# Second routing of a two-layer mixture-of-experts kernel: the four experts of a token from sorted maxima, experts innermost

## The reference, cut to what matters

```python
# _L1_ffn_ref, E = 16, K = 4
logits = hidden_states @ router_w + router_b
probs = jax.nn.softmax(logits, axis=-1)
topw, topi = jax.lax.top_k(probs, K)
topw = topw / jnp.sum(topw, axis=-1, keepdims=True)
combine = jnp.sum(jax.nn.one_hot(topi, E, dtype=hidden_states.dtype) * topw[..., None], axis=2)
...
def body(acc, expert):
    w1e, b1e, w2e, b2e, ce = expert
    hmid = jax.nn.gelu(x @ w1e + b1e, approximate=False)
    return (acc + (hmid @ w2e + b2e) * ce[:, None], None)
```

## Time and profile before

| what | value |
|---|---|
| median of 3 runs | 1959.16 us (1958.06 to 1961.44) |
| the profiled execution | 1959.49 us, its span 1957.8 us |
| PE busy | 1644.8 us, 84% of the span |
| DVE busy | 1159.4 us, 59% |
| ACT busy | 1079.9 us, 55% |
| POOL busy | 659.6 us, 34% |
| second routing, first to last DVE instruction | 1285.03 to 1359.78 us |
| the experts after it, last `join` | to some 1915 us, to 1957.8 us |

### The profile page before, as it was taken

One profiled execution on the slowest core, in us unless ns is written; L12 is line 12 of the kernel. 1 busy time (PEld: TensorE's weight loads), 2 busy tenths in 40 slices (PEclk: granted clock), 3 DMA queues, 4 the chain that ended last, 5 costly groups with the idle time before them and its releaser, 6 DMA issues. The chain is left out here.

```text
span 1957.8 us, 33224 instructions
## 1 busy us (share of the span) xinstructions
PE 1644.8 (84%) x9891; PEld 1111.1 (57%) x9892; DVE 1159.4 (59%) x1934; ACT 1079.9 (55%) x2236; POOL 659.6 (34%) x622
## 2 busy tenths in 40 slices
PE   4989999561699599999999999824999999999990
PEld 2333343250599455444444444512999999999990
DVE  6999998488411264458999999367233333333325
ACT  5888987540133243138887788614455555555554
POOL 0000000130366231211333333211577777777750
PEclk9999999785699799989999999965999999999995
DMA  5000000134121296503333433186344444444427
GB/s 177 1 0 1 0 1 0 47 120 139 41 66 58 85 317 247 71 18 78 78 99 99 100 99 105 33 280 234 53 70 73 68 71 70 65 67 69 69 23 257
DMA packets 145735, 173.67 MB, mean 89 GB/s; under 512 B 29139, under 2 KB 110430, under 8 KB 145504
## 3 DMA queue, kind: packets, MB, share of 16 engines
q1 hardware_dynamic: 104160, 128.29, 21.7%
q0 software_dynamic: 33248, 43.71, 12.8%
q10 hardware_dynamic: 8224, 0.39, 0.2%
HBM read 111.50 MB, written 66.19 MB: 91 GB/s over the span
## 5 line engine op out<-in xcount | busy, mean ns | idle before, releaser
L1323 PEld LDWEIGHTS f_ht_ps<-f_XT,f_WS 128*128 128x128 f32 x2912 | 357.0, 194 | 15.0 <-DVE f_WS L1416 2.6
L1323 PE MATMUL f_ht_ps<-f_XT,f_WS 128*128 128x128 f32 x2912 | 359.9, 277 | 3.0 <-ACT f_XT L1364 3.0
L1331 PE MATMUL f_y_ps<-W,f_HT 128*128 x1456 | 344.1, 379 | 0.0
L1289 POOL DMA_INDIRECT moe<-f_Y,TOK x182 | 276.8, 1521 | 182.6 <-ACT f_Y L1389 146.5
L2151 DVE TENSOR_REDUCE att_MX<-att_s_ps 128x2 f32<-128x1024 f32 x256 | 304.5, 1216 | 53.2 <-PE att_s_ps L1915 53.0
L2116 ACT ACTIVATE att_PT<-att_st_ps 128x512 f32<-128x512 f32 x512 | 278.7, 594 | 69.7 <-PE att_st_ps L1940 59.5
L1331 PEld LDWEIGHTS f_y_ps<-W,f_HT 128*128 128x128 f32 x1456 | 262.6, 190 | 28.3
L1280 POOL DMA_INDIRECT XG<-x,TOK x182 | 191.9, 1054 | 196.2 <-issue 126.0
L1416 DVE COPY f_WS<-W 128x1024 f32 x182 | 133.4, 733 | 203.3 <-PE f_ht_ps L1323 126.3
L1424 DVE TENSOR_TENSOR f_Y<-f_y_ps,f_B 128x256 f32<-128x256 f32 x143 | 60.7, 425 | 296.4 <-PE f_y_ps L1331 296.4
L303 PE MATMUL rec_ring<-rec_XC,rec_W 128*128 128x512 f32 x384 | 183.6, 632 | 50.8 <-DVE rec_XC L353 21.5
(11 more groups left out here) (276 smaller groups left out, 2198.9 us busy)
## 6 DMA issues: line engine op xcount, KB each, us to landing
W<-in_w SPq DMA_DIRECT2D x48, 512.0 KB, 10.0
att_Q<-qk_pairs SPq DMA_DIRECT2D x192, 64.0 KB, 2.9
att_K<-qk_pairs SPq DMA_DIRECT2D x192, 64.0 KB, 2.9
qk_pairs<-prj_HI SPq DMA_DIRECT2D x16, 512.0 KB, 3.8
qk_pairs<-prj_LO SPq DMA_DIRECT2D x16, 512.0 KB, 5.1
hidden<-in_xT SPq DMA_DIRECT2D x8, 512.0 KB, 7.8
x<-n_Y SPq DMA_DIRECT2D x8, 512.0 KB, 3.0
prj_X<-x SPq DMA_DIRECT2D x8, 512.0 KB, 9.1
```

Of the source, the lines that this page charges most:

```text
L1289: nc.gpsimd.indirect_dma_start(out=outs[n % len(outs)], out_offset=bass.IndirectOffsetOnAxis(ap=TOK[:, n:n + 1], axis=0), in_=Y[n % R][:], ...
L1323: mm = nc.tensor.matmul(ht_ps[r % 2][:, f * P:(f + 1) * P], WS[r % 2][:, at:at + P], XT[r % 2][:, c], start=(c == 0), stop=(c == DC - 1))
L1331: mm = nc.tensor.matmul(y_ps[r % 2][:], HT[r % 2][:, f], W2[:, bass.ds(e * W_EXPERT + f * D, D)], start=(f == 0), stop=(f == FC - 1))
```

## The change

Only the K = 4 path of `route` is rewritten; K = 1 keeps its instructions. The probabilities, the masks and the counts are now stored with the token tile outside and the expert inside (`PJ`, `GJ`, `TJ`, `NJ`, `SJ`, `KEEPJ`, shape `[P, TILES, E]`).

- In place of the four rounds, 32 `max` instructions (one for each tile, 16 elements in and the 8 largest in falling order out) write `TOP`; the fourth of them is the least chosen probability. `GJ` marks the experts above it, `TJ` those equal to it, `NJ` counts the equal ones along the experts by a scan (with `KEEPJ`, zero at the first expert of a tile), and so many of them are taken as there is room for. `SJ` is the mask.
- `SEL` is a copy of `SJ` with the axes exchanged, for PE. `begin_count` waits for the copy alone and not for PE; that wait stands now behind the work on `CB` and behind a second scan, which numbers the chosen experts of a token 1 to 4.
- The slot of the k-th choice comes from one instruction (number equal k + 1, times slot) and a sum; the k-th choice is now the k-th by expert number and no longer by probability.
- POOL writes two patterns more (`KEEPJ` and its zero column), in front of `IOTA`. It now waits for all that it wrote before, where it waited for one; that holds for K = 1 too.
- Several instructions are no longer chained to the one ahead.

```diff
--- before.py
+++ after.py
@@ -866,11 +866,16 @@
     with ExitStack() as ctx:
         st = Stage(nc, ctx, tag)
         big = [P, E, TILES]
-        PR = st.sb("PR", big)
-        V = st.sb("V", big)
+        wide_j = [P, TILES, E]
         SEL = st.sb("SEL", big)
-        OH = [st.sb(f"OH{k}", big) for k in range(K)]
-        A = st.sb("A", big)
+        if K == 1:
+            PR = st.sb("PR", big)
+            V = st.sb("V", big)
+            OH = [st.sb("OH0", big)]
+            A = st.sb("A", big)
+        else:
+            PJ, GJ, TJ, NJ, SJ, KEEPJ = (st.sb(name, wide_j) for name in ("PJ", "GJ", "TJ", "NJ", "SJ", "KEEPJ"))
+            TOP = st.sb("TOP", [P, TILES, 8])
         A2 = st.sb("A2", big)
         KEEP = st.sb("KEEP", big)
         WE = st.sb("WE", [P, E, 1])
@@ -956,7 +961,9 @@
         s_dve = st.sem("dve_chain")
         block = ctx.enter_context(nc.Block())
         TURNS = TILES * K // SLOTS_AT_ONCE
+        SETTINGS = 4 if K == 1 else 6
         flat = lambda t: t[:].rearrange("p e j -> p (e j)")
+        by_token = lambda t: t[:].rearrange("p j e -> p (j e)")
         over_j = lambda t: t.unsqueeze(2).to_broadcast(big)
         over_e = lambda t: t.unsqueeze(1).to_broadcast(big)
 
@@ -981,8 +988,12 @@
             nc.gpsimd.memset(KEEP[:], 1.0).then_inc(s_set, 1)
             nc.gpsimd.iota(WE[:, :, 0], [[-1, E]], base=E, channel_multiplier=0, allow_small_or_imprecise_dtypes=True).then_inc(s_set, 1)
             nc.gpsimd.memset(onesE[:], 1.0).then_inc(s_set, 1)
-            pool.wait_ge(s_set, 1)
+            if K > 1:
+                nc.gpsimd.memset(KEEPJ[:], 1.0).then_inc(s_set, 1)
+            pool.wait_ge(s_set, SETTINGS - 1 - (K > 1))
             nc.gpsimd.memset(KEEP[:, :, 0:1], 0.0).then_inc(s_set, 1)
+            if K > 1:
+                nc.gpsimd.memset(KEEPJ[:, :, 0:1], 0.0).then_inc(s_set, 1)
             nc.gpsimd.iota(IOTA[:], [[1, WIDE], [0, SLOTS_AT_ONCE]], base=0, channel_multiplier=0,
                            allow_small_or_imprecise_dtypes=True).then_inc(s_iota, 1)
             st.clear_old(pool)
@@ -1056,6 +1067,12 @@
             def after(ins):
                 own.after(ins)
 
+            def begin_count(ins):
+
+                step[0] += 1
+                ins.then_inc(s_mask, 1)
+                dve.wait_ge(s_mask, step[0])
+
             def counted(ins):
 
                 step[0] += 1
@@ -1077,7 +1094,7 @@
                 after(v.tensor_tensor(out[:], A[:], over_e(m2[:]), ALU.is_equal))
 
 
-            dve.wait_ge(s_set, 4)
+            dve.wait_ge(s_set, SETTINGS)
             after(v.tensor_scalar(AT[:], C["token"][:], float(T // 2), None, ALU.is_gt))
             after(v.tensor_scalar(TV[:], C["token"][:], float(-T // 2 - 1), None, ALU.add))
             after(v.tensor_tensor(TV[:], TV[:], AT[:], ALU.add))
@@ -1094,7 +1111,10 @@
             dve.wait_ge(s_exp, 1)
             after(v.tensor_reduce(m1[:], LB[:], AX.X, ALU.add))
             after(v.reciprocal(m2[:], m1[:]))
-            after(v.tensor_tensor(PR[:], LB[:].rearrange("p j e -> p e j"), over_e(m2[:]), ALU.mult))
+            if K > 1:
+                after(v.tensor_tensor(PJ[:], LB[:], m2[:].unsqueeze(2).to_broadcast(wide_j), ALU.mult))
+            else:
+                after(v.tensor_tensor(PR[:], LB[:].rearrange("p j e -> p e j"), over_e(m2[:]), ALU.mult))
 
             if K == 1:
 
@@ -1150,20 +1170,28 @@
                 counted(v.tensor_copy(SEL[:], OH[0][:]))
                 v.tensor_tensor(CB[:].rearrange("p j e -> p e j"), OH[0][:], PR[:], ALU.mult).then_inc(s_comb, 1)
             else:
-                after(v.tensor_copy(V[:], PR[:]))
-                for k in range(K):
-                    best(V, OH[k])
-                    after(v.scalar_tensor_tensor(out=flat(V), in0=flat(OH[k]), scalar=-2.0, in1=flat(V), op0=ALU.mult, op1=ALU.add))
-                after(v.tensor_tensor(A[:], OH[0][:], OH[1][:], ALU.add))
-                for k in range(2, K - 1):
-                    after(v.tensor_tensor(A[:], A[:], OH[k][:], ALU.add))
-                counted(v.tensor_tensor(SEL[:], A[:], OH[K - 1][:], ALU.add))
-                after(v.tensor_tensor(CB[:].rearrange("p j e -> p e j"), SEL[:], PR[:], ALU.mult))
+                for j in range(TILES):
+                    ins = v.max(TOP[:, j], PJ[:, j])
+                after(ins)
+                least = TOP[:, :, K - 1:K].to_broadcast(wide_j)
+                v.tensor_tensor(GJ[:], PJ[:], least, ALU.is_gt)
+                after(v.tensor_tensor(TJ[:], PJ[:], least, ALU.is_equal))
+                v.tensor_reduce(m1[:], GJ[:], AX.X, ALU.add)
+                after(v.tensor_tensor_scan(by_token(NJ), by_token(KEEPJ), by_token(TJ), 0.0, ALU.mult, ALU.add))
+                after(v.tensor_scalar(m2[:], m1[:], -1.0, float(K), ALU.mult, ALU.add))
+                after(v.tensor_tensor(NJ[:], NJ[:], m2[:].unsqueeze(2).to_broadcast(wide_j), ALU.is_le))
+                after(v.tensor_tensor(TJ[:], TJ[:], NJ[:], ALU.mult))
+                after(v.tensor_tensor(SJ[:], GJ[:], TJ[:], ALU.add))
+                begin_count(v.tensor_copy(SEL[:], SJ[:].rearrange("p j e -> p e j")))
+                v.tensor_tensor(CB[:], SJ[:], PJ[:], ALU.mult)
+                after(v.tensor_tensor_scan(by_token(NJ), by_token(KEEPJ), by_token(SJ), 0.0, ALU.mult, ALU.add))
+                v.tensor_tensor(NJ[:], NJ[:], SJ[:], ALU.mult)
                 after(v.tensor_reduce(m1[:], CB[:], AX.X, ALU.add))
                 after(v.reciprocal(m2[:], m1[:]))
-                v.tensor_tensor(CB[:], CB[:], m2[:].unsqueeze(2).to_broadcast([P, TILES, E]), ALU.mult).then_inc(s_comb, 1)
-
-
+                v.tensor_tensor(CB[:], CB[:], m2[:].unsqueeze(2).to_broadcast(wide_j), ALU.mult).then_inc(s_comb, 1)
+
+
+            dve.wait_ge(s_count, step[0])
             rank_of(RANK)
             after(v.tensor_scalar(pick[:], A2[:, :, TILES - 1], float(P - 1), None, ALU.add))
             after(v.tensor_scalar(pick[:], pick[:], 7, None, ALU.arith_shift_right))
@@ -1171,10 +1199,18 @@
             after(v.tensor_tensor_scan(cumt[:], onesE[:], ntile[:], 0.0, ALU.mult, ALU.add))
             after(v.tensor_tensor(base[:], cumt[:], ntile[:], ALU.subtract))
             after(v.tensor_scalar(base[:], base[:], float(P), None, ALU.mult))
-            after(v.tensor_tensor(RANK[:], RANK[:], over_j(base[:]), ALU.add))
-            for k in range(K):
-                after(v.tensor_tensor(A[:], RANK[:], OH[k][:], ALU.mult))
-                after(v.tensor_reduce(SF[:].rearrange("p (j k) -> p j k", k=K)[:, :, k], A[:].rearrange("p e j -> p j e"), AX.X, ALU.add))
+            if K == 1:
+                after(v.tensor_tensor(RANK[:], RANK[:], over_j(base[:]), ALU.add))
+                after(v.tensor_tensor(A[:], RANK[:], OH[0][:], ALU.mult))
+                after(v.tensor_reduce(SF[:], A[:].rearrange("p e j -> p j e"), AX.X, ALU.add))
+            else:
+                after(v.tensor_tensor(TJ[:], RANK[:].rearrange("p e j -> p j e"), base[:].unsqueeze(1).to_broadcast(wide_j), ALU.add))
+                for k in range(K):
+                    at = GJ if k % 2 == 0 else SJ
+                    after(v.scalar_tensor_tensor(out=by_token(at), in0=by_token(NJ), scalar=float(k + 1), in1=by_token(TJ),
+                                                 op0=ALU.is_equal, op1=ALU.mult))
+                    ins = v.tensor_reduce(SF[:].rearrange("p (j k) -> p j k", k=K)[:, :, k], at[:], AX.X, ALU.add)
+                after(ins)
             after(v.tensor_copy(SI[:], SF[:]))
             after(v.tensor_scalar(LO_I[:], SI[:], P - 1, None, ALU.bitwise_and))
             after(v.tensor_scalar(HI_I[:], SI[:], 7, None, ALU.arith_shift_right))
```

## The result

The changed kernel takes **1944.93 us** (median of four runs, 1942.08 to 1946.43), where the kernel before took 1958.61 on the same chip. The two medians differ by 13.7 us. The ratio of the two kernels, taken over all these executions, is 0.9922, with a 95% interval of 0.991 to 0.9934: 15.3 us less, between 12.9 and 17.6. The forecast was 1943.3, in a range of 1940.9 to 1948.0.

What follows compares the result with a forecast made beforehand. DVE's chained routing instructions were taken to set the expert stage's start. Gains 15.7 + 1.3 less 0.64 and 0.1 made 16.3; 1959.5 - 16.3 + 0.3 = 1943.5, stated as 1943.3 us at the median, range 1940.9 to 1948.0.

Steps and rivals of the forecast that it cites:

- Rival (e): Experts' start: they do not wait for DVE's chain, gain below 3.9 us, kernel at 1955.3 or more; chance 2%.
- First to third step: DVE's routing up to the mask: `PJ` 0.73 us, the 32 MAX 3.0, the mask with its copy to `SEL` 6.4.
- Fourth step: DVE behind the mask: work on `CB` and numbering takes 4.2 us and covers the 3.65 us wait for PE's count.
- Fifth step: DVE's slots: one strided addition and three instruction pairs, 6.5 us for 7.8, a gain of 1.3.
- Sixth step: POOL's added patterns start `IOTA` 0.64 us later, holding DVE; the added wait loses 0.1 in the first layer.
- The booking of 0.3: Start of the expert stage: `B2` and first gather share DMA engines with the remaining weight loads, a loss of 0.3 us.
- the bound of 1.4 us: Upper limit of that DMA-sharing loss: weight loads end at 1344.9, `TOK` is complete at 1343.5.
- Rival (c): DMA engines decide: weights, `B2` and gather queue, first product up to 1.1 us later, 1944.4 at worst; chance 10%.
- The forecast case: Outcome as worked out, given 41%; PE's clock rises some 10 us after its first transposition, as before.
- Rival (b): PE's clock in the second tile: early rise gains 1.8 us (1941.5), late rise loses 1.8 (1945.1); 15% each.
- Rival (a): DVE's 32 MAX do not overlap: 0.22 us each, 7.0 instead of 3.0, kernel at 1947.3; chance 15%.
- Rival (d): MAX is slow by itself: kernel loses from 0.59 us each, 1980.6 at 1.26 us each; chance 2%.

Runs made afterwards that it cites:

- late load of the biases: Changed kernel, and separately the kernel before, with the 2 MB bias load issued only after PE's first transposed tile: 1937.92 us (ratio 0.9883) and 1955.88 us (0.9972).
- the late patterns: Changed kernel with DVE's wait for POOL's patterns moved from its first instruction to behind the exponential, in both routings: 1942.5 us, a single execution.
- both edits: Changed kernel with the late load of the biases and the late patterns together: 1935.61 us, ratio 0.9882.
- the last version: On top of both edits, SP issues the weight loads ahead of the stores of zeros, awaited only before POOL's second scatter: 1934.22 us, ratio 0.987.
- the load cut in sixteen: Changed kernel with the 2 MB bias load issued at the same place as 16 loads of 128 KB: 1940.9 us, ratio 0.9907.

## Why the prediction was right, point by point

**The bound.** It was DVE's chain, as the rows said. Edits of that chain moved the third tile by what they moved in the chain: +7.7 of MAX gave +7.9, +4.24 gave +4.20, 3.87 of idle time gave 3.99. Rival (e) is out. The expert stage kept its length, 577.2 us for 576.9.

**First to third step, up to the mask.** `PJ` took 0.72 for 0.73. MAX took 2.57 with its gap (1295.54 to 1298.11) for 3.0; the row of the four BATCH_NORM_AGGREGATE was the right neighbour, and a little dear (0.095 against 0.079). Its 0.38 us divided by four holds one tail in four, which the forecast took as the price of the longer operand. The trace gives 0.148 to 0.182 us for each of the four, so their starts lie some (0.38 - 0.15) / 3 = 0.077 us apart, and 32 of those with one tail make 2.5. The 0.4 us too much are tails counted eight times; a price of the longer operand doesn't show. The mask took 6.20 (1298.11 to 1304.31) for 6.4, because the copy with exchanged axes costs 0.59 and 0.04 of gap, not 0.79.

**Fourth step.** The work behind the mask took 4.18 us (1304.31 to 1308.49) for 4.2, and the count was there 0.57 us early, forecast at 0.5. With the wait put back, 3.87 us of idle time came back.

**Fifth step.** 6.46 us for 6.5.

**Sixth step.** `zeros` to `AT` grew by 0.64, exactly as priced, and `AT` ended again just behind `IOTA` (1290.40 against 1290.36). In the first layer the distance from the memset of `KEEP` to `AT` went from 0.53 to 0.65, 0.12 for 0.1. What I had as the cause, `IOTA`, was too narrow: memsets hold the same kind of instruction as well.

Together the chain is 17.66 us shorter where 17.0 were priced; the 0.66 are MAX (0.4), the copy (0.15) and roundings.

**What is late next.** The booking of 0.3 was small, and so was what came (0.06), but its working had a wrong step. I had the weights in place at 1344.9, where the traffic falls off. With the late load of the biases, where it can be seen by itself, that traffic ends about 61.4 us behind `zeros` again, yet DVE's copy started 64.14 behind it there, and 64.29 in the changed kernel: this load's landing was seen by its waiter 2.7 us or so after the traffic had fallen. In the frame of the kernel before that is 1347.6, not 1344.9, and the bound of 1.4 us on this term was too small; by its own reasoning it should have been 1347.6 - 1343.5 = 4.1. That this cost nothing is luck: PE needed the copy only 1.3 us behind its transposition, and the gather ahead of that, slow beside `B2`, landed at 1355.12. So there was slack, but not of the chain's own: DVE's copies ended at 1352.57 and PE's first products came at 1356.42, 3.9 us later, and the load of biases had held PE up by 4.4. The late load of biases shows it: take those 4.4 us away, and the weights are what PE waits for.

Rival (c) did not come, and the reason given for the 0.3, that `B2` and the gather share the DMA engines with the rest of the weights, held for `B2` alone. From issue to landing it took 7.7 us before and this after the change:

```profile
f_B<-in_b SPq DMA_DIRECT2D x1, 2048.0 KB, 9.1
```

The gather still came 7.50 us after its issue for 7.44. Issued at 1347.12, `B2` landed near 1356.2, behind the transposition. So the first gather does not land only with `B2`, as I had read it in the kernel before, where the two coincided; it is slowed by it.

**The clock.** In the changed kernel the second tile's products lasted 3.75 us, as before. The clock rose within this window (columns as above, granted clock third from the end):

```profile
1364.00:1366.00 2.00, 2.00 (x12) 1.97 (x12) 0.00 (x0) 0.26 (x1) 0.00 (x0) 0.59 0.00 0
```

By its 0.59 that is at about 1365.6, 10.5 us behind PE's first transposition, where it was 10.4 before. The forecast case held. Rival (b) was a real one all the same, and its 1.8 us right in size: the late load of biases in both kernels, the late patterns, both edits and the last version had the early rise (first to third hidden products 8.9 to 9.3 us instead of 10.7 to 11.2). Of the thirteen profiled executions five had it early and eight late. Which it will be, no row ahead of it told, and PE's idle time before the first transposition does not decide: 7.65 us went with a late rise (the load cut in sixteen) and 7.69 with an early one (both edits).

**The overlap of the MAX.** 32 MAX unchained took 2.53 us, and 6.77 with a wait behind each. So the wait costs 0.133 us each ((6.77 - 2.53) / 32), more than the 0.079 of a MAX without it. Unchained, the next one starts 0.077 us behind the last, for a MAX of 0.156: it starts before its predecessor has ended, as the earlier trace rows had it for the four BATCH_NORM_AGGREGATE. Rival (a) is out, and its price was good: 4.24 us for the 4.0 that it gave. Rival (d) is out with it: it needed 0.59 us a MAX.

**The time.** The changed stretch gave 16.9 us where the forecast counted 16.0 for it. The first median, 1944.93, still stands 1.6 above the forecast, the second, 1942.61, 0.7 below. Between executions of one kernel the first layer's expert stage jumps by 2.1 us, and with it goes most of the difference. By that jump alone, a range narrower than some 2 us was hardly to be had for this kernel.

**What stays open.** Whether the load cut in sixteen frees the gather by its smaller pieces or by its later issues, and why only by 2.6 of 4.4 us; what decides the early or late rise of PE's clock at the start of a stage; and the 1.4 us of the 3.48 ahead of the routing that the first layer's expert stage doesn't account for.

## What to carry to other kernels

Price a short instruction by the distance between starts of the nearest short ones that follow unchained, with one tail for the whole group, and count waits as well as instructions: 32 results that nobody needs one by one cost 0.079 us each with one wait behind the last, and 0.212 with a wait behind each. When a chain sets a stage's start, ask for another engine's result as late as the work allows, which was 4 us here, and then read every load that is issued beside the first small transfer of the next stage: a 2 MB load that nobody needed yet cost as much again. Compare stretches between marks inside the execution when the whole time jumps by 2 us from causes elsewhere; the stretch repeated to 0.1 us.

## What the runs showed of the hardware that I had not expected

**A stage of 146 us has two lengths.** The first layer's expert stage took 145.96 to 145.97 us or 147.8 to 148.1, in the same kernel too. In all thirteen profiled executions, the long one had PE's granted clock at 0.50 in the second tile and the short one at 1.00.

**A small gather beside a large load.** The first gather took 7.5 us from issue to use beside a 2 MB load with 16 KB in a row, 4.9 beside the same bytes in sixteen loads with 1 KB in a row, issued over 7.5 us, and 3.1 to 3.5 without the load.

**A load is seen late.** With the late load of the biases the weights' last traffic ended about 61.4 us behind `zeros`, and the instruction that waited for it started at 64.14, about 2.7 us later. So the end of the DMA share in a window was no landing time here.

**POOL's memsets hold a TENSOR_SCALAR of DVE.** One of 128x32 that takes 0.18 us by itself took 1.07 and 0.57 beside memsets and 1.25 beside `IOTA`, each ending within 0.04 us of POOL's instruction. A TENSOR_TENSOR of 128x512 beside `IOTA` took its usual 0.69.
